# A transformer block with FiLM on one core: the scores of the first query tile are put in front of the last G projection

## The reference

```python
h = film(rmsnorm(x, norm1_w), cond, film1_w, film1_b)
Q = h @ q_w + q_b
K = h @ k_w + k_b
V = h @ v_w + v_b
scores = jnp.einsum('bnd,bmd->bnm', Q, K) * D ** (-0.5)
attn = jax.nn.softmax(scores, axis=-1)
out = jnp.einsum('bnm,bmd->bnd', attn, V)
x = x_in + (out @ proj_w + proj_b)
x_in = x
h = film(rmsnorm(x, norm2_w), cond, film2_w, film2_b)
h = jax.nn.gelu(h @ mlp_w1 + mlp_b1, approximate=False) @ mlp_w2 + mlp_b2
return x_in + h
```

## Time and profile before

| | us |
|---|---|
| median of 3 runs | 233.45 |
| lowest and highest | 233.01 and 233.62 |
| the profiled execution, its own time | 233.46 |
| its span, first to last instruction | 231.6 |

### The profile page before, as it was taken

How to read it: one execution, slowest core, us unless ns; L and a number is a source line. 1 busy time by engine, 2 the same in 40 slices (tenths; PEclk the granted TensorE clock), 3 DMA queues, 4 the chain that set the end, 5 groups by cost and what they waited for, 6 DMA issues and landing times.

```text
span 231.6 us, 3460 instructions
## 1 busy us (share of the span) xinstructions
PE 217.1 (94%) x1260; PEld 188.4 (81%) x1260; DVE 150.4 (65%) x291; ACT 111.2 (48%) x207; POOL 71.1 (31%) x102
## 2 busy tenths in 40 slices
PE   0898999997999999999999889999999999999994
PEld 0777988885999999999999779888688868888994
DVE  0599767588899988899877683146624672436223
ACT  3168654254345455414565850494349424744440
POOL 1575852001664117444243516042203230200000
PEclk9999999999999999999999999999999999999999
DMA  5994000057867786733674404000520042002002
GB/s 169 340 410 171 3 16 29 3 187 253 232 172 252 249 273 227 238 103 141 213 247 146 164 13 171 3 0 0 189 85 0 0 167 106 3 0 91 0 3 91
DMA packets 17873, 29.86 MB, mean 129 GB/s; under 512 B 2112, under 2 KB 11840, under 8 KB 17728
## 3 DMA queue, kind: packets, MB, share of 16 engines
q1 hardware_dynamic: 15552, 21.25, 28.7%
q10 hardware_dynamic: 2304, 8.39, 9.5%
HBM read 17.58 MB, written 12.06 MB: 128 GB/s over the span
## 4 chain that ended last, share of the span: by engine, by line
PE 71%; DVE 13%; DMA 6%; issue 5%; ACT 2%; SPq 2%; ACTq 0%; DVEq 0%
PE psum L761 32%; PE psum L835 18%; PE psum L890 7%; PE psum L882 5%; PE psum L888 4%; DMA raw<-in_film_wT_dram 3%; PE psum L779 3%; DMA keys_first<-crossing 2%; DVE xn L538 2%; DVE probsT L658 2%; PE psum L773 2%; DVE hT L561 1%; DVE x_rows L727 1%; DMA crossing<-turned 1%; PE psum L753 1%
## 5 line engine op out<-in xcount | busy, mean ns | idle before, releaser
L706 DVE TENSOR_TENSOR G_all<-probs,G_all 128x512 fp32r<-128x512 f32 x32 | 22.0, 697 | 47.4 <-ACT G_all L489 47.4
L835 PEld LDWEIGHTS psum<-V_all,probsT 128*128 128x128 f32 x384 | 47.4, 188 | 5.5 <-DVE probsT L658 4.4
L835 PE MATMUL psum<-V_all,probsT 128*128 128x256 f32 x384 | 48.3, 282 | 3.3 <-DVE probsT L658 3.3
L761 PE MATMUL psum<-hT,w 128*128 128x512 f32 x192 | 49.0, 392 | 0.0
L761 PE MATMUL psum<-hT,G_all 128*128 128x512 f32 x192 | 46.5, 392 | 0.0
L489 ACT ACTIVATE probs<-psum,vcol 128x512 f32<-128x512 f32 x32 | 22.0, 689 | 47.1 <-PE psum L761 46.7
L761 PEld LDWEIGHTS psum<-hT,w 128*128 128x128 f32 x192 | 35.4, 188 | 6.7
L761 PEld LDWEIGHTS psum<-hT,G_all 128*128 128x128 f32 x192 | 35.1, 188 | 7.1
L430 ACT CAST probsT<-keys_first 128x1024 fp32r<-128x1024 f32 x16 | 16.8, 1049 | 36.9 <-DVE raw L651 17.7
L335 POOL TENSOR_TENSOR x_rows<-x_rows,add_row 128x256 f32<-128x256 f32 x16 | 11.8, 736 | 67.5 <-DVE probsT L658 67.5
L890 PE MATMUL psum<-w,G_all 128*128 128x512 f32 x84 | 30.6, 398 | 0.0
(11 more groups left out here) (72 smaller groups left out, 256.8 us busy)
## 6 DMA issues: line engine op xcount, KB each, us to landing
keys_first<-crossing SPq DMA_DIRECT2D x64, 128.0 KB, 3.0
crossing<-turned ACTq DMA_DIRECT2D x8, 512.0 KB, 3.8
crossing<-raw ACTq DMA_DIRECT2D x8, 512.0 KB, 3.6
out_dram<-x_rows SPq DMA_DIRECT2D x8, 256.0 KB, 2.6
x_rows<-in_x_dram SPq DMA_DIRECT2D x3, 512.0 KB, 9.6
rows_crossing<-raw SPq DMA_DIRECT2D x3, 512.0 KB, 2.6
raw<-rows_crossing SPq DMA_DIRECT2D x12, 128.0 KB, 2.8
raw<-in_film_wT_dram SPq DMA_DIRECT2D x2, 512.0 KB, 8.5
```

The lines of the kernel that those rows point to most:

```text
L706: dve.tensor_tensor(gelu[:, m, LO, :], gelu_full[:, m % 2, :], gelu[:, m, HI, :].bitcast(F32), ALU.subtract).then_inc(gelu_ready, 1)
L761: last = pe.matmul(dst, stationary(a, k), moving(b, k), start=(n == len(tiles) * len(PASSES) - 1), stop=(n == 0))
L835: last = pe.matmul(bank(6 + t % 2, D), probsT[:, t % 2, a, k, :], V_all[:, t // KT * KT + k, s, :], start=(n == 0), stop=(n == KT * len(PA ...
```

## The change

It reorders three engines' lists and adds and removes no operation. PE does scores 0 as soon as group 2's V tiles are through, then the G projection of group 3, three V tiles, scores 1, the last V tile, and scores 2. ACT does exponential 0 in front of the high parts of G for group 3, and three high V tiles in front of exponential 1. DVE does row maximum 0 and turn 0 in front of the low parts of G for group 3, and three low V tiles before row maximum 1.

```diff
@@ -409,7 +410,8 @@
                 high_V(g - 1)
                 if g == 1:
                     squares(3, GT // 2)
-                high_G(g)
+                if g + 1 < GROUPS:
+                    high_G(g)
@@ -468,9 +470,13 @@
-                if t in (1, 2):
-                    high_V(GROUPS - 1, range(2 * t - 2, 2 * t))
+                if t == 1:
+                    high_V(GROUPS - 1, range(EARLY_V))
+                if t == 2:
+                    high_V(GROUPS - 1, range(EARLY_V, GT))
                 exp(t)
+                if t == 0:
+                    high_G(GROUPS - 1)
                 if t in (0, LAG - 1):
                     store_turned(t)
@@ -631,7 +637,8 @@
                 group_terms(g - 1)
                 if g == 1:
                     squares(3)
-                low_G(g)
+                if g + 1 < GROUPS:
+                    low_G(g)
@@ -673,9 +680,10 @@
                 row_maximum(t)
                 if t == 0:
                     turn_blocks(0)
-                if t in (1, 2):
-                    low_V(GROUPS - 1, range(2 * t - 2, 2 * t))
+                    low_G(GROUPS - 1)
+                    low_V(GROUPS - 1, range(EARLY_V))
                 if t == 2:
+                    low_V(GROUPS - 1, range(EARLY_V, GT))
                     group_terms(GROUPS - 1)
@@ -838,26 +846,23 @@
             pe.wait_ge(qk_ready, 2 * DT)
-            for g in range(GROUPS):
+            for g in range(GROUPS - 1):
                 project_g(g)
...
+            pe.wait_ge(h_done, DT * GROUPS)
+            scores(0)
+            project_g(GROUPS - 1)
+            project_v(GROUPS - 1, range(EARLY_V))
             pe.wait_ge(G_ready, DT * GROUPS)
             scores(1)
-            project_v(GROUPS - 1, range(2))
-            scores(2)
-            project_v(GROUPS - 1, range(2, GT))
-            for t in range(3, TILES):
+            project_v(GROUPS - 1, range(EARLY_V, GT))
+            for t in range(2, TILES):
                 scores(t)
```

More of the change, by code:

```diff
@@ L61, in film_block_kernel @@
     EARLY = 4
+    EARLY_V = 3
     Q = 32
@@ L840, in _ @@
             pe.wait_ge(qk_ready, 2 * DT)
-            for g in range(GROUPS):
+            for g in range(GROUPS - 1):
                 project_g(g)
[L843 to L848, removed]
+                pe.wait_ge(h_done, DT * (g + 1))
+                transpose_rows(g + 1)
                 if g == 0:
@@ L851, in _ @@
                     pe.wait_ge(addrow_ready, 1)
-                if g + 1 < GROUPS:
-                    project_v(g)
+                project_v(g)
+            pe.wait_ge(h_done, DT * GROUPS)
+            scores(0)
+            project_g(GROUPS - 1)
+            project_v(GROUPS - 1, range(EARLY_V))
             pe.wait_ge(G_ready, DT * GROUPS)
             scores(1)
-            project_v(GROUPS - 1, range(2))
-            scores(2)
-            project_v(GROUPS - 1, range(2, GT))
-            for t in range(3, TILES):
+            project_v(GROUPS - 1, range(EARLY_V, GT))
+            for t in range(2, TILES):
                 scores(t)
```

## The result

The changed kernel takes 234.76 us (4 runs, 234.35 to 235.08) against 233.40 us (4 runs, 233.01 to 233.62): ratio 1.0054, interval 1.0035 to 1.0073, or +1.3 us with an interval of 0.8 to 1.7. It is slower, by a little more than the 0.3% that a measurement can tell, and the forecast of 234.6 lies within the interval. The profiled execution took 234.35 us with a span of 232.5.

The account below looks back on a forecast made before the run. PE's work stays; the row maximum, exponential and turn loop, only 0.35 to 0.55 us ahead of the DRAM trip, becomes the later chain before attention 0. Attention 0 moves +1.13: 233.46 + 1.13 = 234.6 us, range 233.8 to 235.3.

Parts of the forecast that it names:

- Step 1: On PE, scores 0 start in the G projection's place at 36.13, 2.86 us earlier; row maximum 0 on DVE at 39.08.
- Step 2: Tile 0's trip through DRAM starts as much earlier, its reload ending near 51.8 instead of 54.65, with 2.9 us to spare.
- The sum: Attention 0 on PE moves from 57.03 to 58.16, +1.13 us, and the end of the kernel moves with it.
- Step 3: Low G on DVE, now behind turn 0, is ready at 44.48; PE gets a new wait of about 0.65 us before scores 1.
- Step 4: Row maximum 1 on DVE starts at 47.49, not 45.91; the loop's first lap grows from 3.97 to 8.41 us.
- Step 5: Two laps of 3.94 us put row maximum 3 at 55.37; scores 4 wait about 0.8 us for exponential 2.
- Step 6: crossed_lo(0) follows the exponential's bias by 0.19 to 0.39 us; PE's wait before attention 0 stays, at about 1.1 us.
- cross-check of the sum: PE's waits added up: 0.65 + 0.8 + 1.1 = 2.55 against 1.34 us before, giving +1.2.
- Rival A: Attention 0 hangs on the DRAM trip alone and follows scores 4 at once; PE loses its 1.34 us wait: 232.1 us; chance 0.04.
- Rival B: ACT and DVE are quicker, scores 1 start at 43.89 behind the V tiles: +0.5 us, 233.9 to 234.0; chance 0.14.
- Rival C: Tile 1's keys come 1.58 us later; a trip 1.4 us longer delays attention 1 by another 0.7: 235.3 us; chance 0.08.

Follow-up runs that it names:

- e2: The changed kernel with DVE's low G of group 3 in front of turn 0: 234.23 us, ratio 1.0031 to the kernel before.
- e3: The changed kernel with the store of turned tile 0 behind the high V tiles, really 0.87 us later: 234.42 us, ratio 1.0038 to the kernel before.
- g2: The changed kernel with the store of turned tile 0 behind exponential 1, really 5.95 us later: 237.07 us, ratio 1.0141 to the kernel before.
- f2: The changed kernel with two V tiles in front of scores 1 in place of three: 234.89 us, ratio 1.0060 to the kernel before.
- e4: The changed kernel with crossed_hi(0) and crossed_lo(0) one tile earlier on ACT and DVE: 233.88 us, ratio 1.0012 to the kernel before.
- f3: The kernel before with group 3's G projection moved behind scores 3, scores 0 and 1 side by side in front: 231.86 us, ratio 0.9929.
- g1: The kernel before with the store of turned tile 0 behind exponential 1, really 1.43 us later: 235.99 us, ratio 1.0081.
- f1: The kernel before with the store of turned tile 0 behind two high V tiles, really 0.1 us later: 233.46 us, ratio 1.0007.

## Why the prediction was right

*Step 1, scores 0 at 36.13, row maximum 0 at 39.08.* 35.99 and 38.91, 2.92 us behind its scores.

*Step 2, the trip starts 2.9 us earlier and has room.* Shown: the store came 3.0 us earlier, e2 and e3 started it 1.9 and 0.9 us late for nothing. The room was undersized: I put it at 2.9 us, g2 at some 4, since the loop's end moved back as well. The sum does not use it.

*Step 3, a wait of 0.65 for low G.* The row says 0.48. A row's idle time starts from the modelled end of the matmul before it, which lies past the pace at which the next could have started. From pace to start it is 44.31 - (41.51 + 2.16) = 0.64 us. e2 removed it and the stretch fell by 0.50.

*Step 4, a first lap of 8.41.* 47.36 - 38.91 = 8.45. f2 and e2 together show which of the two held scores 1 back last: `G_ready` and not the third V tile. That is worth only 0.54 us: in e2 scores 1 start 44.57 - 36.79 = 7.78 us into the stretch, and by then the third V tile has just ended too. The bulk of the lap's growth is the G projection and the three V tiles that now stand between scores 0 and scores 1.

*Step 5, two laps of 3.94 and a wait of 0.8 for exponential 2.* The laps are (55.27 - 47.36) / 2 = 3.96, the wait is 0.64 in the row and 54.12 - (47.88 + 5.47) = 0.77 by the pace.

*Step 6, crossed_lo(0) 0.19 to 0.39 behind the bias, a wait of 1.1 left.* 0.20, the low end. The wait's row says 0.80, and I had put 0.9 to 1.4 as what would show me right; by the pace it is 57.95 - (54.12 + 2.74) = 1.09. The size was right and the yardstick was wrong: I forecast times from pace to start and named them as a row's idle time. The same mix is in the cross-check of the sum, 2.55 against 1.34: 1.34 is a row's idle time, and by the pace the wait before was 57.03 - (50.06 + 5.47) = 1.50. So that check should have said +1.05, and measured it is 0.64 + 0.77 + 1.09 - 1.50 = +1.00.

*The sum.* +1.13 forecast, +1.06 in the profiles, +1.3 (0.8 to 1.7) in the runs.

*Rival A, the head start arrives,* is out in this order, by e2, e4 and g2. The Trainium skill's rule (DMA: Bandwidth & Descriptors, section Rules for kernel authors) to issue a DMA early and wait late was followed by the change, and it lost. f3 shows the condition: the same 2.9 us are worth 1 us of the stretch once the work beside the DMA starts as early as the DMA does.

*Rival B, the V tiles cover low G,* did not happen by itself; e2 is that case made by hand, at 234.23 where B said 233.9 to 234.0.

*Rival C, tile 1's keys late,* did not happen. `crossed_hi(1)` ran at 59.73, against 59.23, and was let go by the DMA as before. I had moved it by the full 1.58 us; the store of tile 1 moved by 1.48 and the trip took 1.0 us less. No wait stood in front of attention 1.

## What to carry to other kernels

The chain of work names the last arrival and says nothing of the next; before a transfer is started earlier, work out when its consumer's engine would get there anyway. Here that was 0.35 to 0.55 us earlier than the data, and the edit that gained 3 us for the transfer cost that engine's loop 1.5. An instruction that is moved forward pushes what it passes backward: look who waits for that, and whether it has to be there at all (G of the last group is first read by scores 12, at 99.2 us in the kernel before, and moving it, not the scores, gave the gain).

## What the runs showed of the hardware that was not expected

**A wait of 2.6 us lowered PE's clock in five of eight executions; in no trace did one of 1.3 us.** Windows of g1, the wait and what followed it:

```profile
56.35:58.92 2.57, 0.00 (x1) 0.00 (x1) 1.28 (x2) 2.15 (x3) 0.00 (x0) 1.00 1.03 289
...
60.00:61.00 1.00, 1.00 (x6) 1.00 (x6) 1.00 (x2) 0.55 (x1) 0.92 (x2) 0.50 0.13 27
...
62.00:63.00 1.00, 1.00 (x7) 1.00 (x7) 0.82 (x1) 0.68 (x2) 0.10 (x1) 0.50 0.98 330
...
63.40:66.20 2.80, 2.80 (x15) 2.30 (x14) 2.15 (x5) 0.00 (x0) 2.27 (x3) 1.00 0.74 216
```

The granted clock is 1.00 through the wait, then 0.50, the lower of the two levels, 1.2 GHz, from 60 to 63, while PE is busy all the time, and 1.00 again behind that. It cost attention 0 4.46 - 2.94 = 1.52 us, more than half of the wait's own length. In g2 it is at 0.50 when the wait of 2.59 us ends. Behind the 1.34 us before attention 0 in the kernel before the clock stayed at 1.00, as it did behind the three waits of the kernel after. Even one and the same kernel does not always do it: by the mean granted clock, 0.993 or 1.000, it fell in five of the eight executions of g1 and g2. How long PE waited in those without a profile is not known.

The Trainium skill (TensorE: Matmul & The Clock Gate, section Part 1: The HAM clock gate) says that the throttled state is the default and activity releases it. The return to 1.00 on busy work agrees. The start of the span is less clear: the rows give 1.00 there, behind 6.52 us without a matmul, but the first eight matmuls of the kernel before (258 columns, f32) come (10.12 - 6.52) / 8 = 0.45 us apart and the eight of line 806 (256 columns, f32) (13.20 - 11.47) / 8 = 0.22. That is the pace of the lower level beside a record of the higher one, and no run settles it.

**A DMA issue does not wait for the activation in front of it on ACT's list.** In g1 exponential 1 starts at 48.10 and store 0, next in the list, is issued at 48.11, a microsecond before the exponential ends. The data had been turned by 45.40 + 1.25 = 46.65, so the store did wait for its turn in the list, until the exponential began, but not for the exponential to end. It is the same in g2 (48.88 for both) and behind a high V tile in f1 (46.26 and 46.27) and e3 (43.84 for both), and it made the doses of f1, e3, g1 and g2 smaller than planned. So a store "behind" an activation, whose data is ready, is a store at its start.

**The trip of a tile through DRAM varies.** From the store's issue to `crossed_hi(0)` it took 8.65 us before, 8.22 in f1, 8.4 to 8.5 in g1 and g2, and 10.51 in f3, each in one execution. In all of them the trips of tiles 0 and 1 lie over each other, most in g1 and g2, so that alone does not explain f3.
